# Two-layer attention on one core: GpSimd leaves one group of maxima subtractions to VectorE, with smaller moves of waits, loads and an embedding add

## The reference

```
xn = group_norm(x);  q, k, v = qkv_w @ xn + qkv_b
x  = x + proj_w @ softmax(q^T k / 8) v + proj_b             # layer 0
e  = [freq(row); time(column)]                              # 64 channels, known in advance
q  = x @ Wq[:512] + e @ Wq[512:];  k = likewise with Wk;  v = x @ Wv
y  = x + softmax(q^T k / 8) v @ Wout + bout                 # layer 1
```

## Time and profile before

| | |
|---|---|
| median of three timed runs | 4,218.99 us |
| the profiled execution's own time | 4,219.53 us |
| its span, first to last instruction | 4,217.8 us |
| busy: TensorE, VectorE, ScalarE, GpSimd | 97%, 78%, 66%, 42% of the span |
| attention stages, about | 405 to 1,988 us and 2,505 to 4,086 us |
| granted clock of TensorE, mean | 0.993 |

### The profile page before, as it was taken

The page is one execution under the profiler, slowest core; times in us unless marked ns, Lnnn a source line. Parts: engine busy times, 40 slices in busy tenths (PEclk is TensorE's granted clock), DMA queues, the critical chain, the costliest instruction groups (busy, mean ns, idle before and its releaser), DMA issues. The chain is left out here.

```text
span 4217.8 us, 88347 instructions
## 1 busy us (share of the span) xinstructions
PE 4099.4 (97%) x30024; PEld 1901.6 (45%) x30024; DVE 3278.0 (78%) x4032; ACT 2763.7 (66%) x3557; POOL 1773.6 (42%) x572
## 2 busy tenths in 40 slices
PE   7999999999999999998999989999999999999989
PEld 4554344444444444444555544444444444444445
DVE  3111999999999999997322239999999999999962
ACT  1112888888888888886000018888888888888840
POOL 0000455555555555553100005555555555555520
PEclk9999999999999999999999999999999999999999
DMA  4112000101000000011333220101000000000116
GB/s 176 75 75 94 10 27 19 37 13 32 20 28 22 22 23 26 26 49 51 118 102 127 97 95 9 31 20 32 19 28 24 22 22 26 24 21 30 42 47 215
DMA packets 157932, 208.41 MB, mean 49 GB/s; under 512 B 9008, under 2 KB 144304, under 8 KB 156848
## 3 DMA queue, kind: packets, MB, share of 16 engines
q1 hardware_dynamic: 137712, 179.28, 12.9%
q10 hardware_dynamic: 20160, 28.32, 1.8%
HBM read 113.19 MB, written 94.37 MB: 49 GB/s over the span
## 5 line engine op out<-in xcount | busy, mean ns | idle before, releaser
L589 POOL TENSOR_TENSOR prob<-prob,mx 128x1056 f32<-128x1056 f32 x564 | 1752.6, 3107 | 2237.0 <-DVE prob L589 2237.0
L753 ACT ACTIVATE prob<-psum_att 128x768 f32<-128x768 f32 x1728 | 1353.9, 822 | 938.6 <-PE psum_att L684 535.4
L684 PE MATMUL psum_att<-qst,kst 64*128 64x384 f32 x6912 | 1286.2, 504 | 30.3 <-DMA kst<-qk_scratch 17.8
L769 ACT ACTIVATE prob<-prob 128x1152 f32<-128x1152 f32 x1152 | 1292.9, 1175 | 16.5 <-POOL prob L589 14.5
L695 PE MATMUL psum_att<-prob,vst 128*32 128x384 f32 x13824 | 1239.3, 490 | 0.4 <-issue 0.4
L856 DVE TENSOR_TENSOR run<-psum_att,run 128x768 f32<-128x768 f32 x1152 | 1057.8, 947 | 24.3 <-PE psum_att L684 23.1
L589 DVE TENSOR_TENSOR prob<-prob,mx 128x1248 f32<-128x1248 f32 (+1 forms) x576 | 972.1, 1688 | 0.0
L684 PEld LDWEIGHTS psum_att<-qst,kst 64*128 64x128 f32 x6912 | 621.9, 187 | 575.2 <-issue 174.2
L695 PEld LDWEIGHTS psum_att<-prob,vst 128*32 128x32 f32 x13824 | 393.7, 109 | 718.4 <-issue 529.1
L870 DVE TENSOR_TENSOR two_tiles<-prob 128x768 f32<-128x768 f32 x564 | 534.4, 948 | 0.0
L309 PE MATMUL psum<-xc_l,wq 128*128 128x384 f32 x1536 | 504.0, 489 | 9.9 <-DVE qk_l L406 4.8
(11 more groups left out here) (56 smaller groups left out, 1690.9 us busy)
## 6 DMA issues: line engine op xcount, KB each, us to landing
qk_scratch<-qk_l SPq DMA_DIRECT2D x48, 768.0 KB, 3.5
v_scratch<-vo_l SPq DMA_DIRECT2D x24, 768.0 KB, 3.5
qst<-qk_scratch SPq DMA_DIRECT2D x96, 192.0 KB, 2.4
kst<-qk_scratch SPq DMA_DIRECT2D x96, 192.0 KB, 2.4
vst<-v_scratch SPq DMA_DIRECT2D x96, 192.0 KB, 2.5
att_scratch<-ob ACTq DMA_DIRECT2D x96, 192.0 KB, 1.9
attc_l<-att_scratch SPq DMA_DIRECT2D x24, 768.0 KB, 5.4
x_sb<-in_x SPq DMA_DIRECT2D x8, 1152.0 KB, 14.0
```

Of the source, the lines that this page charges most:

```text
L589: return engine.tensor_tensor(x, x, m, ALU.subtract)
L684: mm = nc.tensor.matmul(psum[:, 2 * k + e, 0:CH], kst[rows, (3 * c + k) * P:(3 * c + k + 1) * P], qst[par][rows, :], start=True, stop=True ...
L753: nc.scalar.activation(prob[par][:, :, s, :], s_banks(k)[:, :, 0:CH], ACT.Copy).then_inc(copied, 1)
L769: nc.scalar.activation(x, x, ACT.Exp, scale=SCALE).then_inc(exp_done, 1)
```

## The change

- **Attention.** GpSimd leaves out group 3 (`ALONE`) of each block; VectorE subtracts all 384 columns of it, and ScalarE's exponentials of that group wait for VectorE alone. TensorE's `broadcast_max` at c = 1 moves behind the scores and counts each of its three pairs of transposes; ScalarE's copies of the maxima wait for one pair each; VectorE's running maximum at c = 1 waits for the pair that goes into its banks. `spread_den` waits for its banks one by one.
- **Stage l1.** No table: VectorE adds the embedding's row part on the way out of PSUM and signals the bank free (`qk_read`), then adds the column part in SBUF, one tile behind. The first output projection comes before the embedding's matmuls, and GpSimd does nothing here.
- **First normalisation.** Tiles of x are loaded in two halves (`XH`), each with its own semaphore.

The diff, cut:

```diff
+XH = 2
+ALONE = 3
 def norm_part(nc, dve, gn, n, j):
-    if j == 0:
-        dve.wait_ge(gn["x_in"][n], 16)
+    if j % (JB // XH) == 0:
+        dve.wait_ge(gn["x_in"][n][j * XH // JB], 16)
...
-                sp.dma_start(gn["x"][:, c, b * HW:(b + 1) * HW], ...)
+                for h in range(XH):
+                    sp.dma_start(gn["x"][:, c, tokens], x_d[c * P:(c + 1) * P, tokens]).then_inc(gn["x_in"][n][h], 16)
...
+            if out_proj:
+                pe.wait_ge(w_in[out_proj["w_at"]], 16)
+                out_tiles(0, 0)
             if emb:
...
                         if m >= 4:
-                            pe.wait_ge(qk_out, MT * i + m - 3)
+                            pe.wait_ge(qk_read, MT * i + m - 3)
...
+            def add_cols(i, m):
+                dve.wait_ge(qk_read, MT * i + m + 1)
+                nc.vector.tensor_tensor(image(qk[half][:, mt, :]), image(qk[half][:, mt, :]), emb_cols(m), ALU.add)\
+                    .then_inc(qk_out, 1)
...
-                            nc.vector.tensor_tensor(qk[half][:, mt, :], qk_bank(m), emb_of(i, m), ALU.add)\
-                                .then_inc(qk_out, 1)
+                            nc.vector.tensor_tensor(image(qk[half][:, mt, :]), image(qk_bank(m)), emb_rows(i, m),
+                                                    ALU.add).then_inc(qk_read, 1)
+                            if m > 0:
+                                add_cols(i, m - 1)
+                            if m == MT - 1:
+                                add_cols(i, m)
...
+        def pool_count(t, c):
+            return (KC - 1) * t + c + (1 if c < ALONE else 0)
             def broadcast_max(t, c):
...
-                mm.then_inc(broadcast, 1)
+                    mm.then_inc(broadcast, 1)
             def spread_den(t):
                 for r in range(3):
+                    bank_free(t + 3, DEN_SPREAD_AT, r)
...
-                    if c == BROADCAST_AT and not before(t, 1) and live(t - 1):
-                        broadcast_max(t - 1, c)
...
                     if c == TURN_AT and not before(t, 1) and live(t - 1):
                         bank_free(t, c, 2)
                         turn(t - 1)
+                    if c == BROADCAST_AT and not before(t, 1) and live(t - 1):
+                        broadcast_max(t - 1, c)
...
-                    act.wait_ge(broadcast, t + 1)
+                act.wait_ge(broadcast, 3 * t + r + 1)
...
-                if not last(t):
-                    act.wait_ge(pool_shifted, group(t, c))
+                if c != ALONE and not last(t):
+                    act.wait_ge(pool_shifted, pool_count(t, c))
...
-                for c in range(KC):
+                for c in [c for c in range(KC) if c != ALONE]:
...
             def maximum(t, par, s):
                 dve.wait_ge(scored, scored_count(slot(t, s)))
+                if s // 3 == BROADCAST_AT and not before(t, 1):
+                    dve.wait_ge(broadcast, 3 * (t - 1) + s % 3 + 1)
...
-                shift_part(nc.vector, par, c, 0, CH if last(t) else SHIFT_DVE).then_inc(dve_shifted, 1)
+                shift_part(nc.vector, par, c, 0, CH if c == ALONE or last(t) else SHIFT_DVE).then_inc(dve_shifted, 1)
```

More of the change, by code:

```diff
@@ L53, in norm_buffers @@
         gn[name + "_sem"] = ctx.enter_context(nc.semaphore(name))
-    gn["x_in"] = [ctx.enter_context(nc.semaphore(f"x_in{n}")) for n in range(N)]
+    gn["x_in"] = [[ctx.enter_context(nc.semaphore(f"x_in{n}_{h}")) for h in range(XH)] for n in range(N)]
     return gn
@@ L196, in qkv_stage @@
         qk_out = sem("qk_out")
+        qk_read = sem("qk_read") if emb else qk_out
         v_done = sem("v_done")
@@ L223, in pairs_of_chunks, with image, emb_rows, emb_cols @@
             pair(NCH // 2 - 1, True)
[L225 to L229, removed]
+        def image(x):
+            return x.rearrange("p (h w) -> p h w", w=SIDE)
+        def emb_rows(i, m):
+            return bufs["emb_parts"][:, m, bass.ds(i % JB * (CH // SIDE), CH // SIDE)].unsqueeze(2)\
+                .broadcast_to([P, CH // SIDE, SIDE])
+        def emb_cols(m):
+            return bufs["emb_parts"][:, m, SIDE:2 * SIDE].unsqueeze(1).broadcast_to([P, CH // SIDE, SIDE])
         @block.sync
@@ L356, in _ @@
                 pairs_of_chunks(act, pair)
[L358 to L363, removed]
         @block.vector
@@ L384, in input_chunk @@
                     d.then_inc(xc_ready, 1)
+            def add_cols(i, m):
+                half, mt = divmod(m, CT)
+                dve.wait_ge(qk_read, MT * i + m + 1)
+                nc.vector.tensor_tensor(image(qk[half][:, mt, :]), image(qk[half][:, mt, :]), emb_cols(m), ALU.add)\
+                    .then_inc(qk_out, 1)
+            input_chunk(0, 0)
             if emb:
                 dve.wait_ge(emb_copied, 1)
[L388 to L392, removed]
-                input_chunk(0, 0)
             def pair(it, last):
@@ L755, in copy_max @@
             def copy_max(t, par, r):
-                if r == 0:
-                    act.wait_ge(broadcast, t + 1)
-                    if not before(t, 2):
-                        act.wait_ge(dve_shifted, group(t - 2, KC - 1))
-                        act.wait_ge(pool_shifted, group(t - 2, KC - 1))
+                act.wait_ge(broadcast, 3 * t + r + 1)
+                if r == 0 and not before(t, 2):
+                    act.wait_ge(dve_shifted, group(t - 2, KC - 1))
+                    act.wait_ge(pool_shifted, pool_count(t - 2, KC - 1))
                 nc.scalar.activation(mx[par][:, :, r * P:(r + 1) * P], s_banks(r)[:, :, CH:512], ACT.Copy)\
```

19 lines of the change are left out of this document (4 added, 15 removed).

## The result

The changed kernel takes 4,276.5 us (median of four runs, 4,276.2 to 4,276.8): 1.0135 times the kernel before, 95% interval 1.0123 to 1.0146. The direction was forecast; the size, 4,235 with a range up to 4,252, was not. From one turn of the maxima (L656, before L653) to the next, a block's period in the middle of a stage is now 32.98 us for 32.26: +0.72 on 90 blocks is 65 us.

A forecast was written before the change was run, and what follows sets the result against it. TensorE and VectorE were both taken as nearly full, so the order inside a block decides. From 4,219.5 us, attention +25.2, second projection -7.9 and first statistics -1.4 gave 4,235 us, range 4,205 to 4,252.

The forecast's parts named there:

- Steps 1 to 3: In attention, VectorE's long subtraction adds 1.10 us before the reduces; group 4's is freed (-1.26); scores at c=1 stall 0.57.
- Step 4: VectorE's first maximum at c=1 waits for the moved transposes, starting 2.61 to 2.84 us after those scores.
- Step 5: From first maximum at c=1 to last at c=3, VectorE takes 11.77 us without waiting; then 2.05 to next block.
- the forecast's loop: Sum of the steps around one attention block: 32.36 to 32.59 us against 32.26, taken as +0.28 a block.
- VectorE didn't catch up: Rival in attention: VectorE catches up, TensorE sets the loop; about -0.02 us a block, 4,208 us; chance 20 in 100.
- the reduces weren't in time: Rival: long subtraction doesn't delay the reduces, both TensorE waits go; -52 us, 4,158 us; chance 12 in 100.
- More is late than I follow: ScalarE's copies late, TensorE's scores at c=2 wait; further 0.15 to 0.3 us a block, 4,249 to 4,262; chance 10 in 100.
- The clock: Rival: short stalls swing TensorE's clock between half and full rate in attention; +213 us, about 4,450; chance 3 in 100.
- -7.9: Second projection's start: table building goes (-7.1 us) and the embedding's matmuls, moved, cover TensorE's 0.80 wait for input.
- -1.4: First normalisation: with half-tile loads, three statistics of 0.47 us each are done when the last half lands.
- the second adds: Stage l1: one more VectorE add per tile, 54 to 91 us in all, hidden in VectorE's 1.95 us wait between tiles.
- 31.68: TensorE's own path in one attention block, in us, without its two present waits (32.26 - 0.42 - 0.16).

The follow-up runs named there:

- e1: Changed kernel, but GpSimd takes its share of group 3 again, all else as changed: 4,223.0 us.
- e2: Changed kernel, but the six transposes of the maxima stand ahead of the scores at c=1 again: 4,298.5 us.
- e9: Changed kernel, but VectorE's long subtraction of group 3 stands behind the three reduces: 4,256.6 us.
- e3: Changed kernel, but the turn of the denominators stands behind the first score pair at c=3: 4,244.5 us.
- e14: Changed kernel, but the denominators are turned into banks 1 to 3, so the turn waits for two ScalarE copies instead of three: 4,267.7 us.
- e16: As e14, with ScalarE's widening of the denominators ahead of its second copy at c=3 instead of its third: 4,244.7 us.
- e4: Attention stages as in the kernel before; only the edits of the first normalisation and of stage l1 kept: 4,211.6 us.
- e12: As e11, with the first pair of the maxima's transposes ahead of the scores at c=1 and the other two behind: 4,187.6 us.
- e11: As e14, but GpSimd takes its share of group 3 again: 4,213.3 us.
- e7: Changed kernel with GpSimd's share of group 3 back and each pair of the maxima's transposes directly ahead of its bank's score pair: 4,220.6 us.
- e15: As e12, with ScalarE's widening of the denominators ahead of its second copy at c=3: 4,171.2 us.

## Why the prediction was right in direction and wrong in size

- **Steps 1 to 3 held.** First reduce S + 14.45 (forecast 14.46); subtraction of group 4 at 1.45 and of no use; scores of step 1 at S + 15.85 (15.93), with a new wait of 0.42.
- **Step 4 held, in part by luck.** M1 stands 2.90 after the scores, just over the 2.61 to 2.84 forecast: the three score pairs take 2.25, not up to 2.21, and VectorE starts 0.22 behind the first transposes, not up to 0.20. The scores came 0.08 early, so M1 is at S + 18.75, where the forecast's sum took 18.72.
- **Step 5 failed**: "It is now late and doesn't wait: 11.77." VectorE still waits 0.20 at step 3 (L860 at 4044.89), and from M1 to M9 it takes 12.05, as before. From M9 to the next S it is 2.17 for 2.05, because the copy behind M9 no longer sets it: from the turn of the denominators on, TensorE runs without a wait, 5.81 to the next S. Together 14.22 for 13.82: 0.40 a block, 36 us of the 41.5 by which the forecast missed. The rest is step 4 (0.03, 3 us) and the outside (8.1 for 9.3).
- **The reason for it.** I treated VectorE's wait for the scores of step 3 as TensorE's pace, which a later VectorE would absorb. But these scores stand behind the turn of the denominators, that waits for ScalarE's third copy of step 2, and ScalarE's chain to it starts at M1: copies and `mx` copies of step 1, two exponentials, three copies. The same lateness came back to VectorE through ScalarE and TensorE. From M1 to the turn it is 8.41 to 8.47 in before, changed, e1, e2 and e9, with M1 anywhere from 17.86 to 18.94. In before this path had under 0.1 us of slack, so of the 0.89 by which M1 is later in the changed kernel 0.86 are in the turn; the period grew by 0.72, since the spread's wait of 0.16 is gone. e3, and e14 with e16, take the turn's wait away by two different edits, and both end on the forecast's loop with the measured M1 (32.64 and 32.63): shown.
- **The rivals.** VectorE didn't catch up, and the reduces weren't in time. "More is late than I follow" had the engine right (ScalarE's copies) and the place wrong (scores of step 2, which start without a wait); I priced it at 0.15 to 0.3 and cut its upper half from the range; it was 0.40. The clock stayed at 1.00 with waits of 0.42 and 0.52 in every block. By the Trainium skill (TensorE: Matmul & The Clock Gate, "A second HAM failure mode: psum-queue depth-cycling") such spells can make it swing; no run here shows it.
- **Outside attention** -7.9 and -1.4 were forecast, and e4 shows -8.1 together, the second adds hidden as counted. In e4's trace the start of stage l1 is 8.2 shorter and the first turn of the maxima stands 1.4 earlier, as forecast; where the rest of about 1 us goes was not followed. In the changed kernel's trace the statistics ended 1.29 earlier and the first turn of the maxima only 0.4: the first 64 projection matmuls took 23.33 us there and 22.81 before, and 22.4 to 23.9 over the traces of this case, which is as much as the term itself.

The change costs time because VectorE's 1.1 us stand ahead of the reduces and of M1, which the other engines wait for (behind the reduces, in e9, they still cost 0.35 of the 0.60), while what GpSimd gives back is time of an engine that was busy for 858 of 1,480 us. The moved transposes were a sound idea in half: one pair ahead of the scores, two behind (e12 against e11, -26 us).

## What to carry to other kernels

A wait that "goes away because this engine is late" goes away only if the engine that it waits for isn't driven by the same late event: follow that engine's release back until it leaves the loop. Look in the trace for pairs of end and start on two engines with under 0.1 us between them and no wait shown: they can be second critical paths, and a change that is late by more than that pays for nearly all of its lateness there, as 0.86 of 0.89 here. A gain that fails to appear after a wait is removed is looked for in the in-order queues just behind it, as with the widening that e14 left too little time ahead of a copy.

## What was not expected of the hardware

A run of matmuls of one shape costs more than its matmuls. Score runs of 4, 8 and 12 matmuls take 0.84, 1.49 and 2.14 us from start to the next start, runs of 2, 4 and 6 transposes 0.37, 0.58 and 0.80 (rows of e7, e3, e15 and of the changed kernel). That fits a fixed part of about 0.2 for a run of scores and 0.15 for a run of transposes, an estimate from these rows. What makes it isn't shown: at each border of two runs the tile (64*128 or 128*128 in the rows) and the shape change together. Three alternations in place of one cost 0.69 a block (32.37 in e7, for the 31.68 worked out in the prediction), more than the wait they were to save.
